# A selective scan whose first step sizes are spread by TensorE instead of through DRAM, and whose first convolution taps are twice as wide

## The reference

```python
for k in range(K):                                  # K = 4 taps
    uc = uc + up[:, k:k + L, :] * conv_w[:, k]
uc = jax.nn.silu(uc)
dt, Bm, Cm = jnp.split(uc @ xproj, [16, 32], axis=-1)
delta = jax.nn.softplus(dt @ dt_w + dt_b)
def step(h, inp):                                   # 512 channels, 16 states
    h = jnp.exp(d_t[..., None] * A) * h + (d_t * u_t)[..., None] * B_t[:, None, :]
    y_t = jnp.einsum('bdn,bn->bd', h, C_t)
```

## Time and profile before

| | us |
|---|---|
| median of 3 runs | 1528.28 |
| lowest, highest | 1526.73, 1531.03 |
| the profiled execution | 1525.71 |
| its span, first to last instruction | 1523.8 |
| busy in the span: PE, PEld | 1188.0, 664.0 |
| busy in the span: DVE, ACT, POOL | 1152.3, 767.4, 908.1 |

### The profile page before, as it was taken

How to read it: one execution, slowest core, us unless ns; L and a number is a source line. 1 busy time by engine, 2 the same in 40 slices (tenths; PEclk the granted TensorE clock), 3 DMA queues, 4 the chain that set the end, 5 groups by cost and what they waited for, 6 DMA issues and landing times. The chain is left out here.

```text
span 1523.8 us, 14540 instructions
## 1 busy us (share of the span) xinstructions
PE 1188.0 (78%) x4900; PEld 664.0 (44%) x4900; DVE 1152.3 (76%) x1029; ACT 767.4 (50%) x1020; POOL 908.1 (60%) x405
## 2 busy tenths in 40 slices
PE   5999984698738887468987375464577999999998
PEld 4788831233203332123332021121235778787887
DVE  4433355999999999999999999999676554544544
ACT  4434355577546776556675465464245533333440
POOL 4520015999999999999999999999533000000000
PEclk9999995798768999769988696687797999999999
DMA  5133017322373334345222635231104030302012
GB/s 195 43 124 111 28 33 317 152 108 96 117 261 122 125 141 151 124 171 193 102 93 99 234 119 216 114 118 48 57 14 180 0 139 0 139 0 106 18 39 72
DMA packets 42399, 172.16 MB, mean 113 GB/s; under 512 B 5585, under 2 KB 10193, under 8 KB 29282
## 3 DMA queue, kind: packets, MB, share of 16 engines
q1 hardware_dynamic: 42338, 171.41, 30.2%
HBM read 138.36 MB, written 33.03 MB: 112 GB/s over the span
## 5 line engine op out<-in xcount | busy, mean ns | idle before, releaser
L1097 POOL TENSOR_TENSOR scan_dbu<-scan_rep,scan_bc 128x1024 f32<-128x1024 f32 x256 | 596.8, 2358 | 41.4 <-DMA scan_rep<-dd_rows 36.6
L1029 ACT ACTIVATE scan_hs<-scan_rep,scan_neg_a 128x1024 f32<-128x1024 f32 x256 | 285.3, 1118 | 343.2 <-DVE scan_hc L1181 303.8
L1171 DVE TENSOR_TENSOR_SCAN scan_hs<-scan_hs,scan_dbu 128x1024 f32<-128x1024 f32 x192 | 439.0, 2287 | 12.1 <-ACT scan_hs L1029 11.7
L939 PE MATMUL scan_ysum<-scan_hc,scan_sel 128*32 128x512 f32 x1024 | 177.2, 825 | 223.3 <-DVE scan_hc L1181 223.0
L1181 DVE TENSOR_TENSOR scan_hc<-scan_hs,scan_bc 128x1024 f32<-128x1024 f32 x192 | 234.9, 1223 | 6.1
L939 PEld LDWEIGHTS scan_ysum<-scan_hc,scan_sel 128*32 128x32 f32 x1024 | 36.9, 133 | 344.1 <-issue 344.1
L1103 POOL TENSOR_TENSOR scan_hc<-scan_hc,scan_bc 128x1024 f32<-128x1024 f32 x64 | 150.8, 2356 | 11.3 <-DVE scan_hc L1171 10.9
L1171 DVE TENSOR_TENSOR_SCAN scan_hc<-scan_hs,scan_dbu 128x1024 f32<-128x1024 f32 x64 | 145.8, 2278 | 11.4 <-POOL scan_dbu L1097 11.4
L854 PE MATMUL scan_pb<-late_xin,scan_inwf 128*128 128x512 f32 x256 | 114.4, 600 | 0.0
L32 PE MATMUL ffn_sl<-ffn_tanh_s,xm_s 128*128 128x512 f32 x384 | 106.0, 411 | 2.3 <-DVE ffn_tanh_s L1897 2.3
L32 PE MATMUL moe_first<-moe_x_s,moe_w_s 128*128 128x512 f32 x384 | 97.7, 397 | 8.0 <-DVE moe_w_s L412 8.0
(11 more groups left out here) (216 smaller groups left out, 1714.4 us busy)
## 6 DMA issues: line engine op xcount, KB each, us to landing
scan_rep<-dd_rows SPq DMA_DIRECT2D x64, 1024.0 KB, 5.6
scan_bc<-bc_rows SPq DMA_DIRECT2D x32, 512.0 KB, 6.6
dd_rows<-scan_dd SPq DMA_DIRECT2D x16, 1024.0 KB, 3.8
ffn_wt<-in_ew SPq DMA_DIRECT2D x16, 1024.0 KB, 7.0
scan_inwf<-fold SPq DMA_DIRECT2D x12, 512.0 KB, 3.9
cond<-scan_bc SPq DMA_DIRECT2D x16, 256.0 KB, 3.1
y_all<-scan_yo SPq DMA_DIRECT2D x6, 512.0 KB, 3.1
scan_bc<-in_xT SPq DMA_DIRECT2D x4, 512.0 KB, 7.8
```

The lines of the kernel that those rows point to most:

```text
L939: mm = nc.tensor.matmul(ysum[i * D32:(i + 1) * D32, h, :], sel[:], hc[:, (s0 + i) % HCR, h * CT:(h + 1) * CT], start=False, stop=last, til ...
L1029: nc.scalar.activation(hs[:, s % HSR, :], rep[:, e % REPS, 0, :], ACT.Exp, scale=neg_a[:, k % 2, NI * dc + i, r // NI:r // NI + 1]).then_i ...
L1097: nc.gpsimd.tensor_tensor(dbu[:, s % DBR, :], rep[:, e % REPS, 1, :], bc[:, j, 0, :], ALU.mult).then_inc(dbu_done, 1)
L1171: nc.vector.tensor_tensor_scan(states, hs[:, s % HSR, :], dbu[:, s % DBR, :], 0.0, ALU.mult, ALU.add).then_inc(scan_done, 1)
```

## The change

Two things are changed, both for the first sequence only.

The taps of channel group 0 stay in two halves; those of groups 1 to 3 run over 1024 columns, so that there are 5 x 3 = 15 instructions, and `first_silu` waits for the new counts.

The store of `dd` and the four spread loads of period 0 are gone. In their place PE multiplies `dd` by a matrix of zeros and ones, `spread` (128 x 512, in which column c has its one in row c // 4), that is loaded as a third constant into the last `hc` buffer. There are 16 matmuls, for each `i` first du, then delta, each in two halves; they stand at the end of `FRONT`, ahead of the step size of period 1, `skip` and `z_gate`. ACT copies each result into `rep` (`replica(i)`) right ahead of `decay(i)`. POOL waits for the du half of a replica only. SP goes on to the other row loads at once. The waits of everything that counts stores of `dd` or uses of replica buffers are moved by one, and DVE waits for the replicas' end before it writes the last `hc` buffer.

```diff
 FRONT = [("u", 0, dc, h) for dc in range(DC) for h in range(HALVES)] + [("x", 0, h) for h in range(HALVES)] + \
-    [("t", 0, 0, h) for h in range(HALVES)]
+    [("t", 0, 0, h) for h in range(HALVES)] + [("r", i, kind, h) for i in range(NI) for kind in (1, 0) for h in range(HALVES)]
...
+FIRST_TAPS = [(0, 0, 1), (0, 1, 2)] + [(dc, 0, HALVES) for dc in range(1, DC)]
+FIRST_TAPS_LO = [1] + [0] * (DC - 1)
...
+        spread = hc[:, HCR - 1, 0:NI * P]
...
+        def wait_rep(eng, e, kinds=range(2)):
+
+            if e < NI:
+                freed(eng, *(("r", e, kind, h) for kind in kinds for h in range(HALVES)))
+            else:
+                eng.wait_ge(rep_in[e % REPS], 16 * (e // REPS + (e % REPS >= NI)))
...
-                sp.wait_ge(dd_out, 16 * (w + 1))
+                sp.wait_ge(dd_out, 16 * w)
...
-            for dst, name in ((ident, "ident"), (sel, "sel")):
-                sp.dma_start(dst[:], a[name]).then_inc(consts_in, 16)
+            for dst, name in ((ident[:], "ident"), (sel[:], "sel"), (spread, "spread")):
+                sp.dma_start(dst, a[name]).then_inc(consts_in, 16)
             store_rows(0)
             load_rows(0, 0)
-            store_step(0)
-            for i in range(NI):
-                load_rep(0, i)
...
+            def replicate(i, kind, h):
+                out, done = claim(("r", i, kind, h))
+                pe.wait_ge((delta_done, du_done)[kind], 1)
+                nc.tensor.matmul(out, spread[:, i * P:(i + 1) * P],
+                                 dd[:, kind, h * CT:(h + 1) * CT], start=True, stop=True).then_inc(done, 1)
...
+                elif kind == "r":
+                    if args == [0, 1, 0]:
+                        pe.wait_ge(consts_in, 3 * 16)
+                    replicate(*args)
...
             def first_silu(dc):
-                act.wait_ge(conv0, (TAPS - 1) * HALVES * (dc + 1))
+                act.wait_ge(conv0, (TAPS - 1) * (FIRST_TAPS.index((dc, FIRST_TAPS_LO[dc], HALVES)) + 1))
...
-                wait(act, dd_out, 16 * w)
+                wait(act, dd_out, 16 * (w - 1))
+                if w == 1:
+                    for key in ((i, kind, h) for i in range(NI) for kind in range(2) for h in range(HALVES)):
+                        ready(act, "r", *key)
...
+            def replica(i):
+                for kind in (1, 0):
+                    for h in range(HALVES):
+                        x, free = ready(act, "r", i, kind, h)
+                        nc.scalar.activation(rep[:, i, kind, h * CT:(h + 1) * CT], x, ACT.Copy).then_inc(free, 1)
...
-                    act.wait_ge(rep_in[e % REPS], 16 * (e // REPS + 1))
+                    wait_rep(act, e)
...
+                    if w == 0 and r < NI:
+                        replica(r)
                     decay(UPP * w + r)
...
-                    pool.wait_ge(rep_in[e % REPS], 16 * (e // REPS + 1))
+                    wait_rep(pool, e, [1])
...
-            pool.wait_ge(consts_in, 2 * 16)
+            pool.wait_ge(consts_in, 3 * 16)
...
+                if s == HCR - 1:
+                    freed(dve, *(("r", i, kind, h) for i in range(NI) for kind in range(2) for h in range(HALVES)))
...
-            for n in range(DC * HALVES):
-                dc, h = divmod(n, HALVES)
-                dve.wait_ge(u0_done, n + 1)
-                freed(dve, ("u", 0, dc, h))
-                own = uc[:, 0, dc, h * CT:(h + 1) * CT]
+            for i, (dc, lo, hi) in enumerate(FIRST_TAPS):
+                dve.wait_ge(u0_done, HALVES * dc + hi)
+                freed(dve, *(("u", 0, dc, h) for h in range(lo, hi)))
+                own = uc[:, 0, dc, lo * CT:hi * CT]
                 for t in range(TAPS - 1):
-                    wait(dve, conv0, (TAPS - 1) * n + t)
-                    nc.vector.scalar_tensor_tensor(own, u0[:, dc, h * CT + t:(h + 1) * CT + t], taps[:, dc, t:t + 1], own,
+                    wait(dve, conv0, (TAPS - 1) * i + t)
+                    nc.vector.scalar_tensor_tensor(own, u0[:, dc, lo * CT + t:hi * CT + t], taps[:, dc, t:t + 1], own,
                                                    ALU.mult, ALU.add).then_inc(conv0, 1)
...
+    "spread": np.repeat(np.eye(P, dtype=np.float32), NG, axis=1),
```

More of the change, by code:

```diff
@@ L953, in _ @@
                     step_size(*args)
+                elif kind == "r":
+                    if args == [0, 1, 0]:
+                        pe.wait_ge(consts_in, 3 * 16)
+                    replicate(*args)
                 elif args[-1] == 0:
                     first_x_proj()
-            pe.wait_ge(consts_in, 2 * 16)
+            pe.wait_ge(consts_in, 3 * 16)
             pe.wait_ge(diag_done, 2 * DC)
```

## The result

The kernel after takes a median of 1525.77 us (1518.62 to 1528.83, 20 runs) against 1528.12 us for the kernel before (1524.78 to 1532.16, 20 runs beside it): a ratio of 0.9977, with a 95% interval of 0.9967 to 0.9986. It is faster by some 0.2%, which lies within the 0.3% that the prediction called no change, and the time lies inside the predicted range. The profiled execution is another story: it took 1525.60 us with a span of 1523.8 us, the very span of before, at a granted clock of 0.878 (before 0.872).

The account below looks back on a forecast made before the run. DVE's scans and products were taken as the bound from 246.33 us on, so an earlier scan shortens the run. Taps +2.0 and replicas -0.9 us took 1528.28 to 1527.2 us, own range 1525.5 to 1529.2, overall 1523.2 to 1531.2.

Parts of the forecast that it names:

- Taps: First taps on DVE: 6 narrow and 9 wide at 1.35 us take 17.0 us, 2.5 us less.
- What arrives of them: At du's end: 2.0 us of the taps' gain arrives, as a slow x projection on PE eats part.
- ACT late by a copy: ACT's copies ahead of the wide taps: costed at nothing; 1.3 us each time if late.
- The cycle of 4.4 us: Replicas: ACT and PE take turns over two banks, 4.4 us for each unit at full clock.
- Waking PE: PE at the first replicas starts at half clock after its rest: 2.3 us lost, lower end 0.
- POOL: Products end at 297.4 us, letting scan 16 come 1.7 us earlier; diagonals beside the first taps cost nothing.
- ACT and the gate: ACT's path through gates and table loads sets scan 5 at 262.4 us, 1.1 us earlier; PE's gate records just in time.
- The sum: At scan 5: 2.0 us from the taps, -0.9 from the replicas, a gain of 1.1 us.
- C: Rival: PE stays at half clock through the replicas; scan 5 14 us late, total 1542 us; chance 0.07.
- B: Rival: nothing arrives; taps leave 0 to 0.7 us, replicas lose 0.9, total 1528 to 1529 us; chance 0.13.
- D: Rival: the shared port holds DVE at the taps for 6.1 us, total 1533.3 us; chance 0.01.
- A: Rival: PE wakes at once and the taps' gain arrives whole, 4.1 us, total 1524.2 us; chance 0.15.

Follow-up runs that it names:

- e1: Kernel before with only the wide taps; store and spread loads kept. Median 1524.70 us, ratio 0.9985 to the kernel before.
- e8: Kernel after run once more, unchanged, for a second profile. Median 1526.42 us, ratio 0.9983 to the kernel before.
- e2: Kernel after with taps of 512 columns throughout, so only the replicas changed. Median 1532.55 us, ratio 1.0024 to the kernel before.
- e3: Kernel after with two throwaway pairs of `skip` matmuls and the real `skip` of period 0 ahead of the replicas. Median 1523.50 us, ratio 0.9969 to before.
- e9: e6 with the du half of replica 2 also copied by DVE, between scans 0 and 1. Median 1520.88 us, ratio 0.9951 to the kernel before.
- e5: Kernel after with three throwaway pairs of `skip` matmuls ahead of the replicas, real `skip` left in place. Median 1522.38 us, ratio 0.9960 to before.
- e4: Kernel after with only the real `skip` of period 0 moved ahead of the replicas. Median 1526.54 us, ratio 0.9989 to the kernel before.
- e10: The same kernel as e5, run again. Median 1523.43 us, ratio 0.9963 to the kernel before.
- e6: e5 with DVE instead of ACT copying the du halves of replicas 0 and 1. Median 1522.41 us, ratio 0.9960 to the kernel before.

## Why the prediction was right, point by point

**Taps: right.** 15 taps in 17.07 us (16.96 in e1 and e8), forecast 17.0. The unseen instruction, 1024 columns wide, took 1.284 us (the nine of them 11.6 us, with 0.6 us of rests: 1.35 each, the lower bound that I took). The row that groups them:

```profile
L1224 DVE SCALAR_TENSOR_TENSOR late_uc<-scan_hc,scan_taps,late_uc 128x1024 f32<-128x1024 f32 x9 | 11.6, 1284 | 0.6
```

**What arrives of them: mis-sized.** "I take 2.0 us" was 2.8 to 3.0. The step that failed was that the x projection would keep "the same slow spell". Its 12 records took 5.33 or 5.34 us in every profile with wide taps, behind a rest of 1.56 or 1.93 us, and 7.03 us in both profiles with narrow ones, before and e2, behind a rest of 2.42 us. I had reckoned where the spell would end, not whether it would come. The rest of the size I had no term for: 2.51 of the 2.84 us are the taps, and 0.33 come from the step size of period 0, which in before stood in a spell of half clock that I hadn't looked at.

**ACT late by a copy: it happens.** I had costed this at nothing, with 1.3 us as its price. In e3 and e9 the taps stalled once, between the narrow and the wide ones, as DVE's timeline of e3 shows:

```profile
204.75 4.79 DVE L1230 SCALAR_TENSOR_TENSOR late_uc<-scan_hc,scan_taps,late_uc 128x512 f32<-128x512 f32 x6 [2.80 <-ACT late_uc L1005]
210.56 12.20 DVE L1230 SCALAR_TENSOR_TENSOR late_uc<-scan_hc,scan_taps,late_uc 128x1024 f32<-128x1024 f32 x9 [1.03 <-ACT late_uc L1005]
```

The code up to there is that of after. In e3 the granted clock was 0.50 from 202 to 204 us, under PE's first projections, and ACT's copies came late; du came 1.04 us later than in e5 (28.50 against 27.46 from the taps).

**The cycle of 4.4 us: right.** The first spacings are 4.40, 4.39 and 4.38 us in after and within 0.01 us of that in e2, e3, e4, e5, e8 and e10, and e6 showed that it is made by the copies.

**Waking PE: right in kind, mis-sized.** "I take 2.3 us", with ends of 0 and 4. The first 12 records took 8.52 us in after, 8.35 in e4, 7.25 in e2 and 7.08 in e8, against 5.64 in e5: 2.9, 2.7, 1.6 and 1.4 us for the same code or nearly so. It is no one number; in after it was 0.6 above what I took, in e8 0.9 below. What sets it is how long the half clock lasts beyond the first record, as the granted clock of the stretches gives it: 6.1, 5.8, 3.4 and 3.0 us in these four, of which about half is lost. I had forecast 4 to 5 us. Why it lasts longer in one execution than in another, the runs don't show.

**POOL: right.** Its diagonals ran under the taps, and it didn't become the bound: the gain is 1.01 us at scan 5 and still 0.93 at scan 16. **ACT and the gate: right.** The gate's 8 records, which had their own waking before (5.76 us), come behind a busy PE now and take 3.60; decay 5 starts at 261.38 us and scan 5 at 262.53, where 262.4 was forecast, held by ACT as foreseen. ACT came to the gate 0.4 us sooner than in my sum and then waited 0.59 us for its second half, a wait that I had put at nothing ("just in time"). The change moves a waking as much as it adds one. **The `bc` loads: right**, nothing waits for them.

**The sum: right by two errors that cancel.** +2.0 - 0.9 = 1.1 us was forecast for scan 5 and 1.01 came; the parts were +2.84 for du and -1.83 for what follows it. In e8 they are +2.98 and -0.40, in all 2.58. So the median gain, 2.35 us between the two medians, or 3.5 us by the ratio, is more than my 1.1; after's profiled execution was one of the dearer wakings.

**The rivals.** C, half clock throughout, is refuted: the clock is 1.00 from 240 us until past scan 5, through PE's rests of 0.60 us between the banks. The swings that the Trainium skill (TensorE: Matmul & The Clock Gate, on PSUM-queue depth-cycling) tells of don't appear in this stream. B (nothing arrives) is refuted at the taps by e1. D, that the port holds DVE for 6.1 us, is refuted: beside POOL's diagonals the six narrow taps took

```profile
L1224 DVE SCALAR_TENSOR_TENSOR late_uc<-scan_hc,scan_taps,late_uc 128x512 f32<-128x512 f32 x6 | 4.6, 770 | 3.1 <-ACT scan_hc L998 2.8
```

770 ns each against 757 in the earlier trace rows, 0.1 us for all six. By the rule of the Trainium skill (SBUF — State Buffer, on the shared port pair) a tap and a diagonal exclude each other for the whole instruction; on DVE's side the rows show far less than that. Only a tap that starts out of a rest, while a diagonal runs, takes longer (0.86 us for 0.75 at 203.34 us in after, 1.44 for 1.285 at 210.56 us in e3). On POOL's side the last section shows larger ones. A (wakes at once and the taps whole) was half right: the taps arrived whole, the waking was dear.

**What stays open.** The medians aren't additive: taps alone -0.15%, replicas alone +0.24%, both together -0.23% and -0.17%, where the sum would be +0.09%. Each of the ratios is known to 0.10 to 0.13%, so the three together have an error of about 0.2% (the root of the sum of their squares), and the gap is 0.26 to 0.32%. Up to scan 16 the milestones nearly add up in one of the two profiles: -2.94 us (e1) and +0.24 (e2) make -2.70, where e8 has -2.47 and after -0.95. The rest lies behind scan 16, and there the granted clock at the gates differs from profile to profile; whether an edit at the start shifts it in a way that repeats, or by chance, these runs don't settle.

## What to carry to other kernels

When small matrix work takes the place of a transfer, price the engine's waking separately: look at how long TensorE has rested when its operand comes, and if it rests, give it something harmless to do up to that moment; here that turned a loss of 0.5 to 1.9 us into a gain of 1.0. The filler can meet the half clock itself and end too late, as in e3 and e9, where that cost 0.8 us of it. Before moving matmuls out of a gap between two others, look at what the gap then does to the clock of what follows. And where two engines pass tiles over two banks in turn, the cycle is the sum of both their times: take the milestone at which the next engine becomes the bound as the measure of the gain, not the first one that comes earlier.

## What the runs showed of the hardware that I had not expected

The same waking differed by 1.4 us between two executions of one program (8.52 and 7.08 us for the same 12 records behind the same rest of 5.97 us). A rest of 0.96 us, behind four records of 17 rows, came ahead of a fall in e3, and one of 0.95 us in e4, while rests of 0.60 us in the stream of replicas never did it and 1.56 and 1.93 us ahead of the x projection didn't either. And in e3 and e9 the clock fell just as the throwaway pairs began, behind a rest of 0.86 us (granted clock 0.67 and 0.73 from 228 to 230 us), while e5, e6 and e10 kept the full clock behind the same work and the same rest. So the length of the rest alone doesn't decide. An unchanged stretch of some 785 us varied by 7.9 us over the profiles, and the one behind it by 4; the places that I looked at were such spells. A single profiled execution is therefore a poor measure of a gain of 1 or 2 us in the total, and a good one of where the gain goes: the distances within a part that is not touched by a clock change repeat to 0.1 us, most of them to 0.02.

And POOL's diagonals take longer beside DVE's taps. One that starts while DVE rests takes 0.60 us (at 209.99 us in e3, at 202.62 us in before 0.61). The eight took 5.99 us in before and 6.00 in e1, where they were done by 208.9 us, all but the first two beside narrow taps; in after they took 6.83 us and in e5 7.64. The groups of POOL in e5 (count, busy us, mean ns, idle before), from 206 to 208.2 us beside narrow taps, and from 208.3 to 212 us beside wide ones:

```profile
L1165 POOL TENSOR_SCALAR scan_diag<-scan_ident,scan_vec 128x128 f32<-128x128 f32 x4 | 3.3, 831 | 0.0
...
L1165 POOL TENSOR_SCALAR scan_diag<-scan_ident,scan_vec 128x128 f32<-128x128 f32 x3 | 3.5, 1194 | 0.0
```

The same diagonal takes 0.83 us beside taps that come every 0.82 us. Of the second row's three one begins under a narrow tap; the two others, beside taps that come every 1.35 us, took 1.44 and 1.32 us. The wide taps take 1.285 us beside POOL as without it, but for the one out of a rest. That looks like one POOL instruction for each of DVE's, with the port rule cited above falling almost wholly on POOL. That it is the port which does this was not tried by itself. It cost nothing here, since the first reader of the diagonals comes at 254 us in after; where POOL's work beside long DVE instructions is on the path, it would.
